# A four-layer transformer on one core: ScalarE takes a share of the softmax's products and of the joint norms, and the experts of both batches run as one stream

## The reference

```python
gating, index = jax.lax.top_k(affinity_T, K)
x_sel = x[b_idx, index]
h = jax.nn.silu(g) * u
contrib = jnp.einsum('beki,eid->bekd', h, Wd) * gating[..., None]
x_out = jnp.zeros_like(x).at[b_idx, index].add(contrib)
```

## Time and profile before

| | |
|---|---|
| time, median of 3 runs (lowest to highest) | 2147.94 us (2147.43 to 2148.8) |
| the profiled execution: time, span | 2145.2 us, 2143.4 us |
| PE busy | 1921.5 us, 90% |
| DVE busy | 1709.2 us, 80% |
| ACT busy | 1400.0 us, 65% |
| POOL busy | 1245.5 us, 58% |
| stage B, from 140 to 1750 us of the span | 1610 us |

### The profile page before, as it was taken

How to read it: one execution, slowest core, us unless ns; L and a number is a source line. 1 busy time by engine, 2 the same in 40 slices (tenths; PEclk the granted TensorE clock), 3 DMA queues, 4 the chain that set the end, 5 groups by cost and what they waited for, 6 DMA issues and landing times. The chain is left out here.

```text
span 2143.4 us, 79777 instructions
## 1 busy us (share of the span) xinstructions
PE 1921.5 (90%) x33524; PEld 1454.4 (68%) x33524; DVE 1709.2 (80%) x3962; ACT 1400.0 (65%) x5039; POOL 1245.5 (58%) x871
## 2 busy tenths in 40 slices
PE   4769999999999999999999999999999984491677
PEld 2348778687786886868868688687786862251455
DVE  5689889698796996979969789698896965787544
ACT  3159779597695985968959689597795961340222
POOL 2258768388584885857858668586683841031000
PEclk8879999999999999999999999999999997795799
DMA  3011112021120211212112121021110100001000
GB/s 113 0 42 42 31 50 58 21 78 35 44 59 22 76 39 36 58 29 73 41 35 57 33 69 44 24 63 40 51 52 17 42 26 13 0 2 60 1 1 20
DMA packets 88224, 85.65 MB, mean 40 GB/s; under 512 B 15392, under 2 KB 83008, under 8 KB 87232
## 3 DMA queue, kind: packets, MB, share of 16 engines
q1 hardware_dynamic: 87872, 80.63, 13.5%
HBM read 25.51 MB, written 1.05 MB: 12 GB/s over the span
## 5 line engine op out<-in xcount | busy, mean ns | idle before, releaser
L1050 POOL TENSOR_TENSOR RN<-N,minus_half 128x8 f32<-128x8 f32 x384 | 632.5, 1647 | 169.3 <-DVE N L978 169.3
L888 ACT ACTIVATE PB<-PS,NMX 128x64 f32<-128x64 f32 x1536 | 469.5, 334 | 30.3 <-DVE NMX L998 30.2
L647 PE MATMUL PS<-WQ,XS 128*128 128x256 f32 x1536 | 434.6, 406 | 7.5 <-SPq L591 5.9
L888 ACT ACTIVATION_READ_ACCUMULATOR PB<-PS,NMX 128x1 f32 x1536 | 344.7, 224 | 0.0
L647 PEld LDWEIGHTS PS<-WQ,XS 128*128 128x128 f32 x1536 | 261.3, 190 | 44.5 <-SPq L591 6.1
L1045 POOL TENSOR_TENSOR RR<-R 128x512 f32<-128x512 f32 x192 | 244.4, 1273 | 78.1 <-DVE QK L1008 78.1
L871 ACT ACTIVATE QKT<-PS 128x512 f32<-128x512 f32 x384 | 229.0, 596 | 87.3 <-PE PS L733 87.2
L1045 POOL TENSOR_TENSOR RR<-R1B,R2B 128x512 f32<-128x512 f32 x192 | 245.0, 1276 | 69.4 <-DVE QK L1008 69.4
L1008 DVE SCALAR_TENSOR_TENSOR QK<-RN,RR 128x512 f32<-128x512 f32 x384 | 261.7, 681 | 0.6 <-POOL RR L1045 0.6
L978 DVE TENSOR_REDUCE N<-SQ 128x8 f32<-128x512 f32 x384 | 259.5, 676 | 0.0
L854 ACT ACTIVATE SQ<-PS 128x512 f32<-128x512 f32 x384 | 237.1, 617 | 8.0 <-PE PS L647 7.7
(11 more groups left out here) (263 smaller groups left out, 3506.2 us busy)
## 6 DMA issues: line engine op xcount, KB each, us to landing
VS<-XB SPq DMA_DIRECT2D x384, 96.0 KB, 2.1
VS<-XB SPq DMA_DIRECT2D x288, 32.0 KB, 1.9
WQ<-in_wqkv SPq DMA_DIRECT2D x40, 192.0 KB, 2.6
WO<-in_wo SPq DMA_DIRECT2D x6, 512.0 KB, 4.2
XS<-XT SPq DMA_DIRECT2D x10, 256.0 KB, 3.5
XS<-XT SPq DMA_DIRECT2D x10, 255.8 KB, 4.2
BIG<-in_wgu SPq DMA_DIRECT2D x1, 2048.0 KB, 8.1
W<-in_w SPq DMA_DIRECT2D x6, 341.0 KB, 3.3
```

The lines of the kernel that those rows point to most:

```text
L647: mm = nc.tensor.matmul(PQ[:, m % 2, j * 256:(j + 1) * 256], XSb[b][:, t0:t0 + P], WQ[:, pair * 384:pair * 384 + 256], start=True, stop=True)
L888: ex = nc.scalar.activation(PB[:, g % 2, u, :], SC[:, h, DH * t:DH * t + DH], ACT.Exp, bias=NMX[:, u:u + 1], accum_out=PSUMS[:, g % 2, u:u ...
L1050: nc.gpsimd.tensor_tensor(RN[:, g % 2, :], N2[:, g % 2, :], minus_half[:, :], ALU.pow)
```

## The change

Three edits, independent of one another.

1. In stage B ScalarE normalises the fourth tile of a step's probabilities, between L871 and L860; VectorE does three.
2. In a norm with two parts ScalarE normalises the first part's tiles, as an activation with scale and bias (for a plain norm VectorE makes the bias `nmr` = -mean x rstd first, in the midst of the second part's statistics); VectorE does the second part alone.
3. The loop over batches of stage D is gone: 16 half-steps, batches in turn for each expert, with addresses known when the program is built. The tokens' layouts and both one-hot tables are held twice, the scatter table is made in two halves of 512 columns through one bank, and one norm with both batches ends the stage.

```diff
+            pn_last = flow("last_tile_of_probabilities_normalised")
@@ tensor, stage B
                             pe.wait_ge(pn_in.sem, pn_in.take())
+                            pe.wait_ge(pn_last.sem, pn_last.take())
@@ scalar, stage B: after the copy of L871, ahead of outputs(g - 4)
+                        if there(g - 1):
+                            k = (g - 1) % 2
+                            act.wait_ge(ro_in.sem, g)
+                            nc.scalar.activation(PB[:, k, 3, :], PB[:, k, 3, :], ACT.Copy, scale=RO[:, k, 3:4])\
+                                .then_inc(pn_last.sem, 1)
                         if there(g - 4) and not feed_forward_at(g - 1):
                             outputs(g - 4)
@@ vector, stage B
-                                PB[:, k, :, :], PB[:, k, :, :],
-                                RO[:, k, :].unsqueeze(2).to_broadcast([P, 4, 2 * WIN]), ALU.mult)\
+                                PB[:, k, 0:3, :], PB[:, k, 0:3, :],
+                                RO[:, k, 0:3].unsqueeze(2).to_broadcast([P, 3, 2 * WIN]), ALU.mult)\
@@ norm, vector
+                            if split and not rms and (k, h) == (1, 0):
+                                dve.wait_ge(rstd_first.sem, rstd_first.take(NH))
+                                nc.vector.scalar_tensor_tensor(nmr[:, :], mvk[0][:, :, 0], -1.0, rstdk[0][:, :],
+                                                               ALU.mult, ALU.mult).then_inc(shift_first.sem, 1)
                     for k, part in enumerate(parts):
-                        for h in range(NH):
-                            normalise(k, part, range(4 * h, 4 * h + 4))
+                        if not split or k > 0:
+                            for h in range(NH):
+                                normalise(k, part, range(4 * h, 4 * h + 4))
@@ norm, scalar
+                    if split:
+                        for t in range(NT):
+                            if rms:
+                                if t % 4 == 0:
+                                    act.wait_ge(rstd_first.sem, rstd_first.take())
+                                nc.scalar.activation(NTOKk[0][:, t, :], parts[0].source(0, t), ACT.Copy,
+                                                     scale=rstdk[0][:, t:t + 1]).then_inc(ntok_first.sem, 1)
+                            else:
+                                if t == 0:
+                                    act.wait_ge(shift_first.sem, shift_first.take())
+                                nc.scalar.activation(NTOKk[0][:, t, :], parts[0].source(0, t), ACT.Identity,
+                                                     scale=rstdk[0][:, t:t + 1], bias=nmr[:, t:t + 1])\
+                                    .then_inc(ntok_first.sem, 1)
@@ stage D, tensor
-            with nc.Fori(0, B) as b:
...
+            RUNS = B * NE
...
+                    def places(n, h):
+                        row = 32 * h + n % B * NE + n // B
+                        nc.tensor.matmul(PS[:, 0, :], identb[0:HR, row:row + 1].to_broadcast([HR, P]),
+                                         RKB[:, :], start=True, stop=True)\
+                            .then_inc(place_ps.sem, 1)
...
+                            tr.then_inc(ht_ps.sem, 1)
+                            pe.wait_ge(hott_in.sem, hott_in.take())
+                            places(n, 1)
...
+                        if now:
+                            pe.wait_ge(hott_in.sem, hott_in.take())
+                        if coming:
+                            places(n + 1, 0)
...
+                    for k in range(4):
+                        nc.tensor.matmul(PS[:, 4 + k, :], ident[:, :], YT[:, 0:HALF], start=True, stop=False)
+                    for n in range(-2, RUNS):
+                        step(n)
+                    for k in range(4):
+                        nc.tensor.matmul(PS[:, 4 + k, :], ident[:, :], YT[:, 0:HALF], start=False, stop=True)
...
-                norm(Part(tokens=lambda t: bank_tiles(6, t), residual=x_batch(b)))
+            norm(*[Part(tokens=lambda t, b=b: bank_tiles(4 + 2 * b, t), residual=x_batch(b)) for b in range(B)])
```

More of the change, by code:

```diff
@@ L197, in mixed_layers_kernel @@
         res_in = flow("normalised_tile_for_residual")
+        rstd_first = flow("rstd_of_first_part_ready")
+        shift_first = flow("shift_of_first_part_ready")
+        ntok_first = flow("normalised_tile_of_first_part_ready")
         class Part:
@@ L209, in norm @@
         def norm(*parts, rms=False, eps=1e-5):
+            split = len(parts) > 1
             with nc.Block() as block:
@@ L223, in _ @@
                         if part.dst is not None:
+                            ready = ntok_first if split and k == 0 else ntok_in
                             for t in range(NT):
-                                pe.wait_ge(ntok_in.sem, ntok_in.take())
+                                pe.wait_ge(ready.sem, ready.take())
                                 tr = nc.tensor.transpose(bank_tiles(4 * k + 2, t), NTOKk[k][:, t, :],
@@ L230, in _ @@
                     ntok_in.settle(pe)
+                    if split and parts[0].dst is not None:
+                        ntok_first.settle(pe)
                 @block.vector
@@ L280, in _ @@
                         f.settle(dve)
+                    if split and not rms:
+                        rstd_first.settle(dve)
+                    if split and parts[0].residual is not None:
+                        ntok_first.settle(dve)
                 @block.gpsimd
@@ L284, in _ @@
                     for k in range(len(parts)):
+                        done = rstd_first if split and k == 0 else rstd_in
                         for h in range(NH):
@@ L288, in _ @@
                             nc.gpsimd.tensor_tensor(rstdk[k][:, cols], vek[k][:, cols], minus_half[:, 0:4],
-                                                    ALU.pow).then_inc(rstd_in.sem, 1)
+                                                    ALU.pow).then_inc(done.sem, 1)
                     var_in.settle(pool)
@@ L803, in settle @@
                     def settle():
-                        for f in (*vs_dma, qk_in, pn_in, sc_free, qkt_in, xs_dma, wq_in, vp_in, o_free,
+                        for f in (*vs_dma, qk_in, pn_in, pn_last, sc_free, qkt_in, xs_dma, wq_in, vp_in, o_free,
                                   layer_pe, shift_in, ntok_in, xn_in, gelu_free, xo_in):
@@ new lines, in mixed_layers_kernel, with _ @@
+            TOKk = [r[:, 0:NT * (D + NE)].rearrange("p (t n) -> p t n", n=D + NE)
+                    for r in (QKT[:, :, :].rearrange("p k s -> p (k s)"), XB[:, :, :].rearrange("p c n -> p (c n)"))]
+            ONEHOTk = [r[:, 0:4, :].rearrange("p a (c n) -> p (a c) n", n=P) for r in (COSL, COSL1)]
+            ONEHOT_Tk = [r[:, 4:8, :].rearrange("p a b -> p (a b)") for r in (COSL, COSL1)]
+            RUNS = B * NE
+            with nc.Block() as block:
+                @block.scalar
+                def _(act):
+                    for b in range(B):
+                        nc.scalar.activation(TOKk[b][:, :, 0:D], XTOK[:, b * NT:(b + 1) * NT, :], ACT.Copy)
+                @block.vector
+                def _(dve):
+                    for b in range(B):
+                        nc.vector.tensor_copy(TOKk[b][:, :, D:D + NE], AF[:, :, b * NE:(b + 1) * NE])
+                    nc.vector.memset(YT[:, 0:HALF], 0.0)
```

242 lines of the change are left out of this document (104 added, 138 removed).

## The result

| | before | after |
|---|---|---|
| time, median (lowest to highest) | 2147.68 us (2147.35 to 2148.8) | 2164.66 us (2163.38 to 2166.15) |
| profiled execution: time, span | 2145.2, 2143.4 us | 2166.15, 2164.3 us |
| DVE busy | 1709.2 us | 1662.6 us |
| ACT busy | 1400.0 us | 1508.7 us |

The changed kernel takes 1.0078 times as long (95% interval 1.0061 to 1.0096): 17 us slower, and 2164 was forecast.

The account below looks back on a forecast made before the run. TensorE's own order was taken to set stage B's step. Steps +40.4, feed-forwards +1.5, norms -13.5 and stage D -12.0 make +16.4 on 2145.2, so 2161.6, and 2.7 for the median gives 2164 us; range 2142 to 2188.

Parts of the forecast that it names:

- Slack 0.13 us behind L860: Stage B: ScalarE's copy L860 may come 0.13 us later before TensorE's L794 notices.
- Price 0.24 us: Stage B: the new 64-column activation delays L860 by 0.24 us, with bounds of 0.19 and 0.30.
- +81 in the forecast: Stage B steps: cost if the skill's budget held, with the activation at 0.35 us and a delay of 0.22.
- +40.4 us for the steps: Stage B: 367 steps each grow 0.11 us, from 3.26 to 3.37; bounds +22 and +62 us.
- The feed-forwards' +1.5: Stage B: in twelve steps with a feed-forward the activation adds 0 to 0.24 us each, +1.5 us together.
- ScalarE's idle ... 0.10 ... does not become the bound: Stage B: ScalarE's idle time per step shrinks from 0.23 to 0.10 us, so ScalarE is not the bound.
- VectorE's product is worth nothing, and its wait grows two- to threefold: Stage B: shrinking the product to 192 columns gains nothing; VectorE's 22.1 us idle before L998 doubles or triples.
- Norms -13.5: Two-part norms: three residual -7.4, two root-mean-square -4.1, four that end transposed -2.0; together -13.5 us.
- Stage D -12.0: Stage D as one stream: gap between batches -20.0, second token copy +1.0, opening +1.7, closing +1.7, joint norm +3.6 us.
- I cost this at 0, +-0.1 us a step: Stage D: the changed order inside a step, with the same matmuls, costs 0, +-0.1 us a step.
- Sum +16.4: Whole kernel: all terms together add 16.4 us to the profiled 2145.2 us, giving 2161.6 us.
- The rivals: Activation fits in, 2122 us, chance 0.12; its whole duration counts, 2197 us, 0.05; ScalarE's norm share doesn't pay, 2178 us, 0.03.

Follow-up runs that it names:

- experiment 1: The changed kernel without its stage B edit, 2125.22 us; and the kernel before with the stage B edit alone, 2184.56 us.
- experiment 4: The changed kernel with two probability tiles on ScalarE instead of one, both behind the copy of the attention output: 2168.95 us.
- experiment 2: The changed kernel with the new activation behind the copy of the attention output instead of ahead of it: 2126.09 us.

## Why the prediction was right, and where not

- *Slack 0.13 us behind L860*: right, 0.132 to 0.137 by three kernels, and in each of them L828 starts 0.05 us after L894's end, in the median. It rested on two rows and the one real wait at the end of the stage.
- *Price 0.24 us*: right, 0.239. The Trainium skill, ScalarE: Activation LUTs, section What ACT_TABLE_LOAD costs, has 186 ns + 0.833 ns an element, 93 for each pointer and 93 of overlap; an estimate from it is 239 ns with and 146 without a pointer, and the runs show both. The budget in the section Rules for kernel authors of the same page of the Trainium skill, +81 in the forecast, is given there for a tight latency and fails here as a price in a queue, against +36.3.
- *+40.4 us for the steps*: the step came out 3.362, not 3.37, and 354 steps have the full length, not 367: 354 x 0.105 = 37.2, which is just what the stretches with and without the edit differ by (1640.60, and 1603.37 in experiment 1). The feed-forwards' +1.5 did not show.
- *"ScalarE's idle ... 0.10 ... does not become the bound"*: right: in the changed kernel's step it is idle for 0.10 us, from the last read's end (1004.27 + 0.25 = 1004.52) to 1004.62. Its room is larger than that idle time: by experiment 4 it needs 3.144 us, so 0.22 of the 3.362 is left, and 0.11 of experiment 2's 3.257.
- *VectorE's product is worth nothing, and its wait grows two- to threefold*: right in kind, 22.1 to 83.6 us on the profile's page, nearly fourfold.
- *Norms -13.5*: -12.4 in their own stretches. The residual term was exact. The transposed norms were mis-sized, -1.2 for -2.0: from the end of ScalarE's tiles to the last copy 2.3 us passed (114.70 and 116.98 at stage B's start, clock 0.50), where 1.7 + 0.3 was reckoned.
- *Stage D -12.0*: -9.6. Up to the first gate-and-up the opening was +1.64 for +1.7 (9.29 and 7.65 us), closing and joint norm +5.4 for +5.3, the second copy of tokens -0.2 for +1.0, since a table load of 1.28 us no longer stands ahead of the first. **The step that failed** is the order inside a step, "I cost this at 0, +-0.1 us a step": it costs 0.23 to 0.26, some 3.4 us over fourteen steps. From the first gate-and-up to the last it is 95.6 us for 112.1, so -16.5 where -20.0 was reckoned. I counted the matmuls, found them the same and let that stand for their time; but the same product of 512 columns costs 0.44 us alone between fp32 products and 0.18 beside its twin, where TensorE waits for ScalarE anyway. The listed sign of it, a step over 6.4 us, came true.
- *Sum +16.4*: the medians differ by 17.0. That closeness is luck: stage B was put some 5 us too high, norms and stage D together took 3.5 us less off than forecast, and the untouched stretches, reckoned at 0, came out 6.7 longer in the one pair of profiled executions. The direction and most of the size are not luck: they follow from the slack and the price.
- *The rivals*: the activation does not fit in (with an immediate it nearly would: step 3.271, though its price is 0.146 us and not the 0.09 of the plain copies' fit); not its full duration counts; ScalarE's share of the norms does pay.

## What to carry to other kernels

An engine's idle time per step says how much work fits in, not where: price a new instruction by its start-to-start distance, and compare it with the slack of the next release behind it in that queue. The same 0.24 us cost 38 us ahead of the copy and nothing behind it. When an order changes and the work doesn't, ask what the moved instruction was hidden behind: where the engine waits anyway it is cheap. And before a few microseconds in an untouched stage are put down to a change, look at that stage in other executions.

## What the runs showed that I had not expected

- A per-partition scale pointer costs ScalarE 0.093 us in its queue over an immediate one (0.239 against 0.146 us for 64 columns).
- In a ScalarE without idle time every activation is recorded some 0.14 us longer at unchanged spacing (0.74 for 0.60 us).
- A lone bf16 product of 512 columns among fp32 ones takes 0.32 us from its start to the next, and the weights behind it are loaded only then ([0.23 <-issue] before L1705). In the pair the second adds 0.21 to the time up to the transpose; how much of either is the change between bf16 and fp32 no run tells.
- The same 16 affinity products took 1.92 or 3.55 us by the clock granted at that moment. The Trainium skill, TensorE: Matmul & The Clock Gate, Part 1, says that the moment at which the clock rises varies with where the first matmul falls, and four of the traces fit that: the granted clock rises 8.8 us after the norm's first statistics in the kernel before and 9.4 to 9.5 in three others. In the other ten it does not rise there at all, and no run shows why. The untouched stretches together differed by up to 8.2 us between executions.
